# Routed expert tiles in another order, with their row addresses read from a table

## The reference, cut to what matters

```python
shared = gelu(x @ W1s + b1s) @ W2s + b2s
rw = softmax(x @ Wr, axis=-1)
topw, topi = top_k(rw, 2)                    # two of eight experts for each token
topw = topw / sum(topw)
h = gelu(einsum('bsd,edf->bsef', x, W1p) + b1p)
priv = einsum('bsef,efd->bsed', h, W2p) + b2p
routed = einsum('bsed,bse->bsd', priv, mask)   # mask holds topw at the chosen experts
return shared + routed
```

## Time and profile before

| what | us |
|---|---|
| median of 3 runs | 1218.14 (1216.13 to 1223.42) |
| the profiled execution, its time | 1212.27 |
| its span, first to last instruction | 1210.6 |
| PE busy in the span | 990.9 (82%) |
| DVE / ACT / POOL busy | 758.5 / 674.5 / 477.8 |
| POOL scatters into slot_rows_in | 128 DMAs, 126.1 busy |

### The profile page before, as it was taken

One profiled execution on the slowest core, in us unless ns is written; L12 is line 12 of the kernel. 1 busy time (PEld: TensorE's weight loads), 2 busy tenths in 40 slices (PEclk: granted clock), 3 DMA queues, 4 the chain that ended last, 5 costly groups with the idle time before them and its releaser, 6 DMA issues. The chain is left out here.

```text
span 1210.6 us, 24580 instructions
## 1 busy us (share of the span) xinstructions
PE 990.9 (82%) x8007; PEld 824.9 (68%) x8007; DVE 758.5 (63%) x2318; ACT 674.5 (56%) x1675; POOL 477.8 (39%) x469
## 2 busy tenths in 40 slices
PE   2788888987999975454999993489898999739998
PEld 1677777775777875454999992266665666428997
DVE  4689999995610333132555552358888887559998
ACT  4456666644343443232556651268788888557774
POOL 2555555550255545552000004667766742201111
PEclk9899999997999988686999996689999999869999
DMA  7801000013432243435666751111111100000111
GB/s 202 333 11 37 35 35 35 36 40 93 135 117 64 59 134 111 122 108 136 178 173 172 174 146 44 44 29 34 33 30 31 32 22 1 1 0 27 35 35 44
DMA packets 92389, 94.70 MB, mean 78 GB/s; under 512 B 16384, under 2 KB 70272, under 8 KB 91136
## 3 DMA queue, kind: packets, MB, share of 16 engines
q1 hardware_dynamic: 81984, 72.43, 21.1%
q0 software_dynamic: 8192, 16.79, 4.8%
q10 hardware_dynamic: 2112, 4.19, 1.3%
HBM read 53.00 MB, written 34.10 MB: 72 GB/s over the span
## 5 line engine op out<-in xcount | busy, mean ns | idle before, releaser
L1525 POOL DMA_INDIRECT g_y<-slot_rows_out,slots x128 | 130.7, 1021 | 229.3 <-SPq L1954 177.9
L1266 POOL DMA_INDIRECT slot_rows_in<-xn_all,slots x128 | 126.1, 985 | 130.6 <-DMA slot_rows_in<-xn_all,slots 80.8
L1162 ACT ACTIVATE s_hT<-s_hp,expert 128x256 f32<-128x256 f32 x288 | 114.0, 476 | 96.3 <-PE s_hp L1153 91.2
L1175 PE MATMUL s_yp<-w_experts,s_hT 128*128 x1152 | 141.5, 277 | 0.3 <-ACT s_hT L1162 0.3
L1175 PEld LDWEIGHTS s_yp<-w_experts,s_hT 128*128 128x128 f32 x1152 | 136.4, 194 | 0.5 <-issue 0.5
L1183 DVE TENSOR_TENSOR xnT_all<-s_yp,expert 128x256 f32<-128x256 f32 x72 | 30.6, 425 | 116.9 <-PE s_yp L1175 109.7
L1138 DVE TENSOR_TENSOR e_wl<-expert,e_wh 128x512 fp32r<-128x512 f32 x72 | 49.2, 684 | 73.8 <-ACT e_wh L1133 72.8
L491 DVE SCALAR_TENSOR_TENSOR l_mi<-l_sbc,mT 128x512 bf16<-128x512 f32 x128 | 86.1, 683 | 12.0 <-PE l_sbc L482 9.7
L1133 ACT CAST e_wh<-expert 128x512 fp32r<-128x512 f32 x72 | 45.2, 629 | 78.7 <-DMA expert<-expert_rows 67.1
L1151 PE MATMUL s_hp<-e_xh,e_wh 128*128 128x256 f32 x288 | 89.0, 309 | 0.0
L1117 PE MATMUL r_prefix<-ident,xnT_all 128*128 128x128 f32 x144 | 28.5, 280 | 67.2 <-DMA xnT_all<-slot_rows_in 65.6
(11 more groups left out here) (320 smaller groups left out, 2769.8 us busy)
## 6 DMA issues: line engine op xcount, KB each, us to landing
expert<-expert_rows SPq DMA_DIRECT2D x72, 322.0 KB
slot_rows_in<-zeros SPq DMA_DIRECT2D x9, 1024.0 KB, 11.8
xnT_all<-slot_rows_in SPq DMA_DIRECT2D x72, 128.0 KB
slot_rows_out<-xnT_all SPq DMA_DIRECT2D x72, 128.0 KB
xn_all<-l_xr SPq DMA_DIRECT2D x16, 256.0 KB, 2.3
xnT_all<-l_rT SPq DMA_DIRECT2D x16, 256.0 KB, 2.3
out_dram<-f_ot SPq DMA_DIRECT2D x16, 256.0 KB, 2.3
w_experts<-in_L_ffn_W2p_dram SPq DMA_DIRECT2D x8, 256.0 KB, 3.8
```

The costliest lines, as they stand in the source:

```text
L1162: nc.scalar.activation(hT[q % 2][:, c, :], hp[:, c, 0:TILE], ACT.Gelu, bias=wt[q][:, F + c:F + c + 1]).then_inc(s["h_ok"], 1)
L1175: ins = pe.matmul(yp[q % 2][:, h * D:(h + 1) * D], hT[q % 2][:, c, h * P:(h + 1) * P], w2, start=(c == 0 and h == 0), stop=(c == FC - 1), ...
L1266: pool.indirect_dma_start(k.rows_in, bass.IndirectOffsetOnAxis(ap=k.slots[:, c, b:b + 1], axis=0), k.xn[:, b, :], None).then_inc(scattered ...
L1525: pool.indirect_dma_start(y_slot[c][:, b, :], None, k.rows_out, bass.IndirectOffsetOnAxis(ap=k.slots[:, c, b:b + 1], axis=0))\
```

## The change

The slots lie expert by expert: expert 0's tiles first, then expert 1's. A tile's block number is therefore no longer its place in the loop. DVE and PE compute, for each tile, a key from the chunk that completes it (times 256) plus its old row-by-row number; the place is the count of smaller keys. `tile_table` gets three rows: expert, block number and chunk. SP reads the block number into a register for each load and each store. The chunk is waited for in the first 48 places, and place 48 waits for all. The expert fetch from tile 6 on moves from SP's queue to ACT's, behind the gelus. The loads no longer wait for the result of the tile six before. There are 71 tile places in place of 72.

```diff
-TILES = -(-(TOPK * BATCHES * TOKENS // TILE + EXPERTS - 1) // 2) * 2
+TILES = TOPK * BATCHES * TOKENS // TILE + EXPERTS - 1
-EARLY = 24
+EARLY = 48
+        def pe_keys(pe):
+            pe.wait_ge(s["keys"], 1)
+            pe.matmul(counts[0:J, 256:256 + J * EXPERTS], k.ones[0:J, 0:J], key_diag[:].rearrange("p n e -> p (n e)"),
+                      start=True, stop=True, skip_group_check=True).then_inc(s["key_ps"], 1)
         def rows_of(ap, t):
-            return ap[t * TILE:(t + 1) * TILE, :].rearrange("(h p) d -> p h d", p=P)
+            return ap[bass.ds(t * TILE, TILE), :].rearrange("(h p) d -> p h d", p=P)
         def sp_load(sp, t):
             q = t % U
+            at = sp.value_load(k.tile_table[1:2, t:t + 1], min_val=0, max_val=TILES - 1)
             wait(sp, s["tp_ps"], t - U + 1)
-            wait(sp, s["y_ok"], t - U + 1)
             if t < EARLY:
-                after = sp.value_load(k.tile_table[1:2, t:t + 1], min_val=0, max_val=CHUNKS - 1)
+                after = sp.value_load(k.tile_table[2:3, t:t + 1], min_val=0, max_val=CHUNKS - 1)
                 sp.wait_ge(s["arrived"], after + 1)
...
-            sp.dma_start(xt[q], rows_of(k.rows_in, t)).then_inc(x_in[q], 16)
-            if t >= U:
-                fetch_expert(sp, k, t, q)
+            sp.dma_start(xt[q], rows_of(k.rows_in, at)).then_inc(x_in[q], 16)
         def sp_store(sp, t):
+            at = sp.value_load(k.tile_table[1:2, t:t + 1], min_val=0, max_val=TILES - 1)
             wait(sp, s["y_ok"], t + 1)
-            sp.dma_start(rows_of(k.rows_out, t), yt[t % U]).then_inc(out[t % U], 16)
+            sp.dma_start(rows_of(k.rows_out, at), yt[t % U]).then_inc(out[t % U], 16)
+        def act_fetch(act, t):
+            wait(act, s["y_ok"], t - U + 1)
+            fetch_expert(act, k, t, t % U)
...
             if more > 0:
                 act_gelu(act, *ahead(i, q, 1))
+            if U <= i * U + q - 1 + U < TILES:
+                act_fetch(act, i * U + q - 1 + U)
...
                 pe_shared_down(pe, 3, 1)
+                pe_keys(pe)
+                pe_shared_up(pe, 5)
+                pe_shared_down(pe, 4, 0)
+                pe_shared_up(pe, 6)
                 pe_table(pe)
...
+                dve.tensor_tensor(earlier[:], em8[:].unsqueeze(2).to_broadcast(EE), em8[:].unsqueeze(1).to_broadcast(EE),
+                                  ALU.is_gt)
...
+                fold(dve.tensor_tensor(upto[:], earlier[:], n_tiles[:].unsqueeze(1).to_broadcast(EE), ALU.mult))
+                chain(dve.tensor_reduce(first_tile[:], upto[:], AX.X, ALU.add))
+                chain(dve.scalar_tensor_tensor(left, first_tile[:].unsqueeze(1).to_broadcast(BE), float(TILE),
+                                               all_before, ALU.mult, ALU.add))
+                dve.tensor_tensor(first[:], first[:], left, ALU.mult)
+                fold(dve.tensor_tensor(second[:], second[:], left, ALU.mult))
+                dve.tensor_reduce(slot_f[:, 0], first[:], AX.X, ALU.add)
+                fold(dve.tensor_reduce(slot_f[:, 1], second[:], AX.X, ALU.add))
+                dve.tensor_copy(k.slots[:], slot_f[:]).then_inc(s["slots"], 1)
...
+                fold(dve.scalar_tensor_tensor(order[:], needs[:], float(J * EXPERTS), order[:], ALU.mult, ALU.add))
+                fold(dve.scalar_tensor_tensor(key[:], valid[:], -USED, order[:], ALU.mult, ALU.add))
+                dve.tensor_scalar(key_low[:], key[:], -0.5, None, ALU.add)
...
+                dve.wait_ge(s["key_ps"], 1)
+                every_key = counts[here, 256:256 + J * EXPERTS].unsqueeze(1).to_broadcast(KEYS)
+                for h in range(2):
+                    mine = slice(h * HALF, h * HALF + HALF)
+                    fold(dve.tensor_tensor(below, every_key, key_low[:, mine].unsqueeze(2).to_broadcast(KEYS), ALU.is_lt))
+                    fold(dve.tensor_reduce(place[:, mine], below, AX.X, ALU.add))
```

More of the change, by code:

```diff
@@ L982, in experts_phase @@
         n_tiles = sb("r_n_tiles", [P, EXPERTS])
[L983 to L985 removed]
+        earlier, upto = sb("r_earlier", EE), sb("r_upto", EE)
+        first_tile = sb("r_first_tile", [P, EXPERTS])
         slot_f = sb("r_slot_f", [P, 2, BATCHES])
[L987 to L989 removed]
+        valid, tile_at = sb("r_valid", [J, EXPERTS]), sb("r_tile_at", [J, EXPERTS])
+        place, marked = sb("r_place", [J, EXPERTS]), sb("r_marked", [J, EXPERTS])
+        order, key, key_low = sb("r_order", [J, EXPERTS]), sb("r_key", [J, EXPERTS]), sb("r_key_low", [J, EXPERTS])
+        key_diag = sb("r_key_diag", [J, J, EXPERTS])
+        below = scratch[0:J].rearrange("p t (e n) -> p (t e) n", n=J * EXPERTS)
         filled, later = sb("r_filled", [J, EXPERTS]), sb("r_later", [J, CHUNKS - 1, EXPERTS])
         needs = sb("r_needs", [J, EXPERTS])
[L992 to L993 removed]
+        payload = sb("r_payload", [J, EXPERTS + 1, 3], BF16)
+        is_tile = sb("r_is_tile", [J, EXPERTS + 1, TILES], BF16)
         pool_fence = sb("r_pool_fence", [P, CHUNKS])
@@ L1016, in experts_phase @@
         s = {n: sem("m_" + n) for n in (
-            "iota", "d", "slots", "table", "tot_ps", "pre_ps", "tab_ps", "arrived",
+            "iota", "d", "slots", "keys", "marks", "table", "tot_ps", "pre_ps", "key_ps", "tab_ps", "arrived",
             "sh_ps", "sh_ok", "sy_ps", "sy_read", "fold",
@@ L1047, in pe_prefix @@
                       skip_group_check=True).then_inc(s["pre_ps"], 1)
+        def pe_keys(pe):
+            pe.wait_ge(s["keys"], 1)
+            pe.matmul(counts[0:J, 256:256 + J * EXPERTS], k.ones[0:J, 0:J], key_diag[:].rearrange("p n e -> p (n e)"),
+                      start=True, stop=True, skip_group_check=True).then_inc(s["key_ps"], 1)
         def pe_table(pe):
[L1050 to L1053, removed]
+            pe.wait_ge(s["marks"], 1)
+            for e in range(EXPERTS + 1):
+                ins = pe.matmul(counts[0:3, 184:184 + TILES], payload[:, e, :], is_tile[:, e, :], start=(e == 0),
+                                stop=(e == EXPERTS), skip_group_check=True)
             ins.then_inc(s["tab_ps"], 1)
@@ L1241, in _ @@
                 for q in range(U):
-                    sp.wait_ge(out[q], 16 * (TILES // U))
+                    sp.wait_ge(out[q], 16 * len(range(q, TILES, U)))
             @block.gpsimd
@@ L1308, in _ @@
                 pe.wait_ge(k.experts_loaded, 16 * k.expert_dmas)
-                pe.wait_ge(s["table"], 2)
+                pe.wait_ge(s["table"], 1)
                 pe_transpose(pe, 0, 0)
@@ L1396, in _ @@
                                        filled[:].unsqueeze(1).to_broadcast([J, CHUNKS - 1, EXPERTS]), ALU.is_lt))
-                dve.tensor_reduce(needs[:], later[:].rearrange("p c e -> p e c"), AX.X, ALU.add)
-                fold(dve.tensor_reduce(in_row[:], ahead_of[:], AX.X, ALU.add))
-                fold(dve.tensor_scalar(place[:], in_row[:], row_at[:], None, ALU.add))
-                dve.tensor_scalar(payload[:, :, 0], em8[here], float(EXPERTS), None, ALU.add)
-                dve.tensor_copy(payload[:, :, 1], needs[:])
+                fold(dve.tensor_reduce(needs[:], later[:].rearrange("p c e -> p e c"), AX.X, ALU.add))
```

69 lines of the change are left out of this document (32 added, 37 removed).

## The result

The changed kernel takes 1150.52 us (median of 4, 1145.94 to 1151.36); the kernel before, run beside it, 1220.59 us. The ratio is 0.9401 (95% interval 0.9371 to 0.9431): 70 us less, where 68.1 was forecast. Chips differ: in the four sets of runs of this study the kernel before took 1220.6, 1208.2 (e1 to e4), 1215.7 (e5 to e8) and 1200.8 us (f1 to f4). The last three sets ran on three different chips; the chip of the first is not on record. So runs are compared with the kernel before on their own chip, by ratio, or by their profiles.

A forecast was written before the change was run, and what follows sets the result against it. PE binds the tile loop, apart from stops where the order asks for late chunks early. Last transpose 655.0 + 0.6 = 655.6 against 723.67 is 68.1 us less: 1218.14 - 68.1 = 1150.0 us, range 1140 to 1168 (8 in 10).

The forecast's parts named there:

- The stops: Tile loop: PE idles before tiles 8, 16 and 24 because the order asks for late chunks early; about 66 us.
- The period of 3.44 us: Tile loop: each tile costs 3.44 us, from ACT's gelus of neighbouring tiles with PE as the releaser.
- The slots 4.7 us earlier: Slot chain before the scatter: shorter steps end it at 317.3 us, 4.7 us earlier; first scatter at 318.2.
- The scatter's pace: POOL's scatter beside the tile loop: 2.15 us per scatter instead of 1.59 alone; last chunk at 575.0 us.
- The wait at place 48: Tile 48 waits for the last chunk, starting at 577.3 us, 4.7 us late, plus a slow restart of 1.96.
- rival A: Tile loop: no wait at place 48 as the scatter is slowed less; 74.8 us less, 1143 us; chance 0.2.
- SP's queue: Tile loop below place 48: three register reads and two DMA issues take 3.10 us, under 3.44; cost 0.
- The fetch on ACT: Tile loop: the expert fetch takes ACT 1.12 to 1.25 us, within 1.36 us idle before its gelus; cost 0.
- rival C: Tile loop: ACT becomes the bound; 6.5 us per 0.1 us of fetch step beyond 1.36, 1172 at 1.7; chance 0.09.
- its form by the page: ACT's fetch with the skill's 600 ns register-load floor: step 1.45 us, 0.09 over idle time, kernel 1156 us.
- The later table and the small matmuls: Before the loop: first expert fetch moves from 338.58 to about 348 us, hidden; small matmuls cost PE 0.6 us.
- What follows the loop: Last tile, gathers, second graph and last layer: unchanged in length, shifting as a whole.

The follow-up runs named there:

- e1: Changed kernel with place 24 instead of place 48 waiting for all 8 chunks (EARLY = 24): 1199.01 us, ratio 0.9926 to the kernel before.
- e4: Changed kernel with SP taking block numbers and chunks as constants in place of its three register reads per tile: 1137.07 us, ratio 0.9424 to the kernel before.
- e5: Changed kernel with SP keeping the load's block number for the store, two register reads per tile instead of three: 1148.8 us, ratio 0.9436.
- e8: Changed kernel with 72 tile places as before instead of 71: 1150.74 us, ratio 0.9468 to the kernel before.
- f1: Changed kernel run again without further edits, on another chip: 1130.13 us, ratio 0.9411 to the kernel before.
- f4: Changed kernel with two more unused register reads ahead of each expert fetch on ACT: 1139.48 us, ratio 0.9495 to the kernel before.
- e2: Kernel before, old order, with only the chunk wait lengthened to place 48 (EARLY = 48): 1210.34 us, ratio 1.0023 to the kernel before.
- e7: Changed kernel with four idle DVE multiplications (4.9 us) ahead of the last slots step: 1148.68 us, ratio 0.9455 to the kernel before.
- e6: Changed kernel with one more unused register read per tile in SP's queue, ahead of the store: 1156.22 us, ratio 0.9496 to the kernel before.
- f2: Kernel before run once more, unedited, on the chip of f1: 1201.2 us, ratio 1.0005 to the kernel before.
- f3: Changed kernel with one SP register read less per tile and place 52 waiting for all chunks (EARLY = 52): 1129.5 us, ratio 0.9402.

## Why the prediction was right, point by point

**The stops.** Right, and this is the gain. PE was bound by the order in which it asked for chunks. The three idle times (65.6 us) are gone, and e1 and e2 show that order and chunk wait are worth nothing or little apart.

**The period of 3.44 us.** Right: 3.434 after tile 48, 3.433 for the whole loop of f1.

**The slots 4.7 us earlier.** Right as a time (first scatter at 318.13, forecast 318.2), and right that it hides (e7).

**The scatter's pace.** 2.15 us were forecast beside the tiles; chunks 4 to 7 took 135.6 us in 64 scatters, 2.12 each. Its last signal came 7 us before the forecast of 575.0. The difference lies ahead of that term: chunk 0 took 29.3 us (318.13 to 347.39) where I had carried over the 35.1 of before (322.90 to 358.03), with the first six fetches now behind it, and chunk 3 took 28.3 us, where I had let the dense traffic begin at 413.

**The wait at place 48.** Forecast at 4.7 us and 2.0 of restart. In the first profile, in f1 and in e7 it cost PE nothing; in e8, e5 and f4 PE waited 2.1, 5.8 and 6.7 us. The last signal lay between 562.7 and 577.6 us in the ten profiles of the sorted order other than e1, around the 571 us that a signal may have if tile 48 is to start freely at 573. So the term is of the right size where it occurs, and can fall either way. For its wait the first profile was the case of rival A, without one.

**SP's queue, "Cost: 0".** Right. The loads were 3.66 us apart on average in the first profile, not 3.10, but every one of tiles 7 to 47 had landed at least 5.7 us before PE needed it, and PE waited for none. With one read more (e6) the queue does cost, as the step of 3.87 us says.

**What the sum didn't have.** The 6.0 us between tiles 5 and 48 stand in no term of the prediction. They followed on products of PE that reached DVE and ACT up to 3.3 us late. In f1 they are absent. The cause stays open.

**The total.** Luck in one part. The sum of 655.6 for the last transpose met 654.49 because these 6.0 us stood in the place of the 6.7 of the wait that didn't come. On the chip of f1 neither occurred, and the loop ended 74.3 us earlier, near rival A's 74.8 and not the 68.1 of the forecast. By ratio both runs (0.9401 and 0.9411) lie between the forecast (0.944) and A (0.938).

**The fetch on ACT.** No cost, as forecast, with more room than I took: 0.56 us from the gelus' end to the next cast (622.56 to 623.12), where I had 1.12 to 1.25. ACT's register read is 287 ns at the median. That is also under the 600 ns that the Trainium skill (DMA: Bandwidth & Descriptors, Latency and other measured facts) gives; rival C and its form by the page did not come.

**The later table and the small matmuls.** Right: first fetch at 347.78 (forecast about 348), tile 5 later by 0.66 us (0.6).

**What follows the loop.** Right, though the first two profiles seemed to deny it. It took pairs on one chip to tell: f1 and f2, and e1 and e2.

## What to carry to other kernels

When a consumer waits for a producer that is nowhere near its own end, look at the order in which the consumer asks: sort it by completion, and let each item wait for its own completion. Either alone may be worth nothing. Before a queue is given more to do per item, add up its own step from the rows of its reads and issues and compare it with the item's period: here 3.10 us fitted into 3.44 and 3.87 did not. Before such a queue is blamed for a delay, look at whether the consumer waited for its transfers at all: uneven or long steps of a queue can be the consequence of a delay elsewhere. And compare stages between profiles of one chip only: a stage that no edit touched took 468.0 us on one chip, 475 on a second and 477.6 to 481.3 on a third, a difference as large as the terms that were in question.

## What had not been expected of the hardware

ACT's register read runs while its gelus do: with one read, 0.12 us pass from the gelus' end to the issue of the DMA, though the read is 287 ns long and has 170 ns of helpers behind it; with three it is 0.82 us. In SP's queue a read of 272 ns with its helpers costs 0.77 us.

On some chips a product of PE reached the engines that wait for it late, while POOL was scattering: bias adds started up to 2.7 us after the product's end in the first profile and in e4 and e5, 2.4 to 3.0 us in e6, e7 and e8. In f1, f3 and f4, of one chip, none was 0.3 us late, at much the same traffic (205 GB/s from 502 to 560 us in f1, 198 from 502 to 570 in the first profile). Behind the last chunk signal none was in any of these profiles. PE loses time only where such a lateness is longer than the room that the loop has: the first profile lost 6.0 us to it, e4 0.6. The cause was not found.

The DMA issues and register reads of SP took uneven steps in the first profile while POOL was scattering (loads 2.3 to 5.6 us apart), and steps of 2.9 to 4.0 us for the same program in f1. Some of them come from stores that waited for a late result; that all do is not shown.
